# Two prepared layouts of x, pixel by pixel and in padded rows, in place of x's transposes and spread row loads

## The reference, cut to what matters

```python
# x: (4, 256, 64, 64) f32
k = conv(x, w1, padding=6, dilation=2) + b1          # 128 channels, 7x7
k = conv(k, w2) + b2                                 # 49 channels, 1x1
attn = softmax(k, axis=1)
xp = pad(x, 6)
shifts = stack([xp[:, :, 2*u:2*u+64, 2*v:2*v+64] for u in range(7) for v in range(7)], axis=1)
x = einsum('bkchw,bkhw->bchw', shifts, attn)         # layer 0 ends
h = relu(bn(conv(x, v1)))                            # 64 channels, 1x1
h = relu(bn(conv(h, v2, padding=1)))                 # 64 channels, 3x3
out = relu(bn(conv(h, v3)) + x)                      # 256 channels, 1x1
```

## Time and profile before

| | |
|---|---|
| time, median of 3 runs (lowest, highest) | 819.55 us (817.19, 820.55) |
| profiled execution: its own time / span of its instructions | 817.85 us / 816.0 us |
| granted TensorE clock, mean | 0.99 of full speed |
| busy: PE, weight loads, DVE, ACT, POOL | 96%, 88%, 81%, 47%, 43% |
| DMA | 162.17 MB in 250108 packets |

### The profile page before, as it was taken

How to read it: one execution, slowest core, us unless ns; L and a number is a source line. 1 busy time by engine, 2 the same in 40 slices (tenths; PEclk the granted TensorE clock), 3 DMA queues, 4 the chain that set the end, 5 groups by cost and what they waited for, 6 DMA issues and landing times.

```text
span 816.0 us, 13800 instructions
## 1 busy us (share of the span) xinstructions
PE 785.2 (96%) x4973; PEld 720.5 (88%) x4973; DVE 663.8 (81%) x909; ACT 381.1 (47%) x663; POOL 349.6 (43%) x253
## 2 busy tenths in 40 slices
PE   6989999999999999999999999999998999999996
PEld 2369999899999999999999999999997987777785
DVE  5998998897799588868986996888658777978896
ACT  3642212343344434444443444353425777728586
POOL 3345654484268238624852682376220012515300
PEclk9999998999999999999999999999999999999999
DMA  9951236957994899499669958784797879805598
GB/s 308 324 178 29 52 81 164 237 148 204 181 253 106 236 179 249 108 241 189 167 177 201 227 138 236 143 226 112 204 175 210 269 221 296 345 1 203 204 373 354
DMA packets 250108, 162.17 MB, mean 199 GB/s; under 512 B 191881, under 2 KB 232826, under 8 KB 247226
## 3 DMA queue, kind: packets, MB, share of 16 engines
q1 hardware_dynamic: 241322, 141.83, 67.0%
q10 hardware_dynamic: 8720, 19.47, 7.3%
HBM read 99.48 MB, written 56.36 MB: 191 GB/s over the span
## 4 chain that ended last, share of the span: by engine, by line
PE 79%; DVE 10%; issue 4%; ACT 2%; DMA 2%; POOL 1%; SPq 0%; DVEq 0%; ACTq 0%; POOLq 0%
PE ps L1338 22%; PE ps L1340 22%; PE ps L1339 22%; PE ps L1455 4%; PE ps L1505 3%; PE ps L1471 3%; DMA xbuf<-in_x 1%; DVE wsum L1828 1%; PE ps L1733 1%; DVE wpart L1828 1%; DVE whole L1878 1%; POOL ring L875 1%; PE ps L1725 1%; DMA w1raw<-in_L_conv_w 1%; DVE logit L1971 1%
## 5 line engine op out<-in xcount | busy, mean ns | idle before, releaser
L875 POOL TENSOR_TENSOR ring<-whole,ring 128x576 fp32r<-128x576 f32 x112 | 196.5, 1760 | 285.1 <-ACT ring L957 285.1
L1338 PE MATMUL ps<-w_hi,ring 128*128 128x336 f32 x832 | 276.9, 333 | 3.6 <-POOL ring L875 3.6
L1340 PE MATMUL ps<-w_hi,ring 128*128 128x336 f32 x832 | 264.3, 318 | 0.0
L1339 PE MATMUL ps<-w_lo,ring 128*128 128x336 f32 x832 | 263.1, 316 | 0.0
L1338 PEld LDWEIGHTS ps<-w_hi,ring 128*128 128x128 f32 x832 | 158.8, 191 | 9.6 <-issue 6.1
L1339 PEld LDWEIGHTS ps<-w_lo,ring 128*128 128x128 f32 x832 | 158.6, 191 | 0.0
L1340 PEld LDWEIGHTS ps<-w_hi,ring 128*128 128x128 f32 x832 | 157.8, 190 | 0.0
L957 ACT ACTIVATE ring<-whole 128x576 fp32r<-128x576 f32 x112 | 87.0, 783 | 88.0 <-POOL whole L870 45.6
L957 ACT ACTIVATE band_hi<-ps 128x320 fp32r<-128x320 f32 (+1 forms) x128 | 53.0, 418 | 125.7 <-PE ps L1455 117.6
L1338 PE MATMUL ps<-band_hi,xT_hi 128*128 128x224 f32 (+2 forms) x320 | 94.7, 296 | 2.9 <-DVE logit L1971 1.7
L1339 PE MATMUL ps<-band_lo,xT_hi 128*128 128x224 f32 (+2 forms) x320 | 92.3, 288 | 0.0
(11 more groups left out here) (229 smaller groups left out, 1360.1 us busy)
## 6 DMA issues: line engine op xcount, KB each, us to landing
xq<-in_x SPq DMA_DIRECT2D x108, 256.0 KB, 4.6
raw<-bands SPq DMA_DIRECT2D x32, 768.0 KB, 7.0
xbuf<-in_x SPq DMA_DIRECT2D x16, 1024.0 KB, 8.8
x_dram<-x ACTq DMA_DIRECT2D x31, 512.0 KB, 5.7
bands<-wide SPq DMA_DIRECT2D x64, 199.0 KB, 4.8
x1in<-x_dram SPq DMA_DIRECT2D x6, 2048.0 KB, 21.1
out<-x1in SPq DMA_DIRECT2D x12, 1024.0 KB, 3.9
bands<-wide SPq DMA_DIRECT2D x3, 1792.0 KB, 11.3
```

Source lines behind the costliest of these rows:

```text
L875: pool.tensor_tensor(split(k, 1), positions(whole[:, k % TBUFS, :], 0, 2), split(k, 0).bitcast(F32), ALU.subtract).then_inc(sig_lo_done, 1)
L1338: pe.matmul(dst, l_hi, r_hi_, start=first, stop=False, **kw)
L1339: pe.matmul(dst, l_hi, r_lo_, start=False, stop=False, **kw)
L1340: return pe.matmul(dst, l_lo, r_hi_, start=False, stop=last, **kw)
```

## The change

`kernel()` gives the program x twice. `x_rows` holds for each i the 128 partitions' 32 rows of 72 with the zeros in place, `x_pixels` holds for each step eight tiles of 128 pixels by 256 channels. In the program:

- `load_x` is one plain copy of 2310 numbers per partition. The memsets of zeros and `pads`, with the waits for them, are gone.
- `x_T` is gone on PE, with its turns of PSUM banks. `load_xp(g, pt)` loads the tile pair of part `pt` into `xp`, one of four slots (one DMA in place of two), after DVE has used what was in it; for steps 14 and 15 to the free parts of `xbuf` (`xp2`).
- ACT's `xT` copies and DVE's `xT` subtracts from `xp` or `xp2` in SBUF instead of from PSUM. Parts 2 and 3 of step 13 are split in `drain(13)` and no longer in the last half.

```diff
-        xq = sb(l0b, "xq", [P, 2, CB, 8, W])
+        xp = sb(l0b, "xp", [P, 4, 2, C])
...
+        def xp_of(g, pt):
+            return xp2(pt)[:, g - DRAIN - 1, :, :] if g > DRAIN else xp[:, pt, :, :]
...
-                src = x[n, cb * P:(cb + 1) * P].rearrange("p (r a) w -> p r a w", a=2)[:, :, a, :]
-                sp.dma_start(xflat(i)[:, 0:SH * XC].rearrange("p (r c) -> p r c", c=XC)[:, :, 2 * PAD:2 * PAD + W], src
-                             ).then_inc(x_loaded[i % XBUFS], 16)
+                sp.dma_start(xflat(i), x_rows[i]).then_inc(x_loaded[i % XBUFS], 16)
...
-                elif g == DRAIN:
-                    sp.wait_ge(xt_done, x_count(g, pt + 2))
-                elif pt >= 2:
-                    sp.wait_ge(xt_done, x_count(g, pt - 2))
-                elif g:
-                    sp.wait_ge(xt_done, x_count(g - 1, pt + 2))
+                    for i in range(2):
+                        sp.dma_start(xp2(pt)[:, i, :, :], x_pixels[g + i, 2 * pt:2 * pt + 2].rearrange("t p c -> p t c")
+                                     ).then_inc(xp2_loaded[pt], 16)
+                    return
+                if g:
+                    sp.wait_ge(xT_lo_done, x_count(g - 1, pt))
...
+                sp.dma_start(xp[:, pt, :, :], x_pixels[g, 2 * pt:2 * pt + 2].rearrange("t p c -> p t c")).then_inc(xp_loaded[pt], 16)
...
-            def pads(i):
...
             def xT(g, pt):
-                act.wait_ge(xt_done, x_count(g, pt))
+                wait_xp(act, g, pt)
                 wait_xT(act, g, pt)
-                copy(xT_pair(g, pt)[0], turn_bank("x", g, pt).rearrange("p (t c) -> p t c", c=C)).then_inc(xT_hi_done, 1)
+                copy(xT_pair(g, pt)[0], xp_of(g, pt)).then_inc(xT_hi_done, 1)
...
-            def x_T(g, pt):
...
-                    if i >= XBUFS:
-                        dve.wait_ge(pads_done, 3 * (i - XBUFS + 1))
...
-                minus(lo, turn_bank("x", g, pt).rearrange("p (t c) -> p t c", c=C), hi.bitcast(F32)).then_inc(xT_lo_done, 1)
+                minus(lo, xp_of(g, pt), hi.bitcast(F32)).then_inc(xT_lo_done, 1)
...
+    rows = x.reshape(B, CB, P, SH, 2, W).transpose(0, 4, 1, 2, 3, 5)
+    rows = np.pad(rows, [(0, 0)] * 5 + [(2 * PAD, XC - W - 2 * PAD)]).reshape(2 * PAIRS, P, SH * XC)
+    given["x_rows"] = np.pad(rows, [(0, 0), (0, 0), (0, XLEN - SH * XC)])
+    given["x_pixels"] = x.reshape(B, C, SH, 2, SW, 2).transpose(0, 3, 5, 2, 4, 1).reshape(STEPS, NT, P, C)
```

More of the change, by code:

```diff
@@ L452, in late, with xp2, wait_xp @@
             return 2 * g + h >= 2 * DRAIN - 1
-        def xq2(pt):
+        def xp2(pt):
             at = XLEN - 1024 * (2 - pt % 2)
-            place = xbuf[:, 1 + pt // 2, at:at + 1024]
-            return place.rearrange("p (k r c) -> p k r c", k=CB, c=W)
+            return xbuf[:, 1 + pt // 2, at:at + 1024].rearrange("p (i t c) -> p i t c", i=2, c=C)
+        def xp_of(g, pt):
+            return xp2(pt)[:, g - DRAIN - 1, :, :] if g > DRAIN else xp[:, pt, :, :]
+        def wait_xp(eng, g, pt):
+            if g > DRAIN:
+                eng.wait_ge(xp2_loaded[pt], 32)
+            else:
+                eng.wait_ge(xp_loaded[pt], 16 * (g + 1))
         def raw_of(g, t):
@@ L521, in x_count @@
         def x_count(g, pt):
-            if g == DRAIN - 1 and pt >= 2:
-                return 4 * g + 2 * pt - 1
-            if g == DRAIN:
-                return 4 * g + (3 + pt if pt < 2 else 2 * pt - 4)
             return 4 * g + pt + 1
@@ L739, in half @@
                 if image is not None:
-                    load_xq(image, 2)
+                    load_xp(image, 2)
                 last = q == 2 * PAIRS - 1
@@ L743, in half @@
                     for pt in range(2):
-                        load_xq(DRAIN + 1, pt)
+                        load_xp(DRAIN + 1, pt)
                 elif q % 2 == 1 and conv is not None:
@@ L765, in half @@
                     if coming:
-                        load_xq(coming, 0)
+                        load_xp(coming, 0)
                     load_raw(coming, 0)
@@ L773, in half @@
                     if coming:
-                        load_xq(coming, 1)
+                        load_xp(coming, 1)
+                    if last:
+                        load_xp(coming, 2)
                     load_raw(coming, 1)
+                    if last:
+                        load_xp(coming, 3)
                 if q == 2 * PAIRS - 1:
@@ L848, in _ @@
             pool.memset(bias[:, :], 0.0).then_inc(consts, 1)
-            for c0, c1 in ((0, 2 * PAD), (2 * PAD + W, XC)):
-                pool.memset(xbuf[:, :, 0:SH * XC].rearrange("p i (r c) -> p i r c", c=XC)[:, :, :, c0:c1], 0.0).then_inc(consts, 1)
-            pool.memset(xbuf[:, :, SH * XC:XLEN], 0.0).then_inc(consts, 1)
-            pool.wait_ge(consts, 11)
+            pool.wait_ge(consts, 8)
             for i, off in enumerate((0, 64, -64)):
@@ L1098, in image_part @@
                     xT(image, part // 3)
-                    if part == 8 and image == DRAIN - 1:
-                        xT(DRAIN, 2)
                 if part == 6:
@@ L2057, in image_part @@
                     xT(image, (2, 6, 9).index(part))
-                    if part == 9 and image == DRAIN - 1:
-                        xT(DRAIN, 2)
                 if part in (7, 8):
```

116 lines of the change are left out of this document (27 added, 89 removed).

## The result

The changed kernel takes 805.32 us (median of 4 runs, 803.32 to 806.52) against 818.73 us (817.19 to 820.55) of the kernel before on the same chip: a ratio of 0.9832, 95% interval 0.9807 to 0.9858. It gains 13.4 us where 26.7 were forecast. The profiled execution took 806.52 us, the longest of the four, at a mean granted clock of 0.982; the other three had 0.988 to 0.991.

A forecast was written before the change was run, and what follows sets the result against it. The prediction took TensorE's issue to bound the steady state: 817.85 - 26.9 (transposes) - 1.2 (start) - 0.6 + 1.0 (moved subtractions) + 1.0 (SBUF reads) = 791.1, plus 1.70 to the median, 792.8 us; range 785 to 804.

The forecast's parts named there:

- The sign and the pairs' work: Whole kernel faster, chance 0.95; in the steady pairs, TensorE's time falls from 75.2 to 71.5 us, 0.46 per transpose group.
- The start: First load of x lands sooner, so VectorE's first operation starts earlier: -1.2 us, within 0 to 1.7.
- VectorE and ScalarE read SBUF in place of PSUM: +1.0 us: In the split of x, xT_lo costs 0.4 us more each, VectorE's pair reaches 64.6 us: +1.0 us overall.
- the lock: VectorE instructions with two SBUF inputs and GpSimd instructions reading SBUF block each other: up to 1.25 us more per xT_lo.
- Only those on the chain count: 3.3% of 816.0: Over the whole span, removed TensorE transposes gain only their share of the chain of waits: -26.9 us, about 58 groups.
- the sum: All terms added to the profiled 817.85 us give 791.1; with 1.70 to the median, 792.8 us.
- The second: Rival: in the pairs VectorE and GpSimd block each other and TensorE waits; half the gain goes, 805 us; chance 0.17.
- VectorE was not the bound: Judges the slower rival: VectorE becomes the bound in the pairs, 81.4 us each, 855 us in all; chance 0.03.

The follow-up runs named there:

- e8_rows: The kernel before with the padded rows of x alone and without the memsets, its transposes kept: 818.8 us, ratio 0.9989.
- e1_psum: Changed kernel, but ScalarE copies each piece of xp into a PSUM bank and VectorE subtracts from there, except in steps 13 to 15: 802.73 us, ratio 0.9786.
- e3_xt2: Changed kernel with ScalarE's and VectorE's split of part 2 moved ahead of the softmax's end in every half: 800.36 us, ratio 0.9758.
- g2_xt2b4: As e3_xt2, and also band_lo of tile 4 moved ahead of the whole before it on VectorE: 798.32 us, ratio 0.9748.
- f2_fill: Changed kernel with four matmuls without use in place of each group of transposes, from the last half on: 809.91 us, ratio 0.9886.
- g1_fill2: Changed kernel with two matmuls without use in place of each group of transposes, from the last half on: 804.35 us, ratio 0.9834.
- e2: Changed kernel with GpSimd's operations on xbuf for a pair's first buffer moved one chunk later: 823.21 us, ratio 1.0048.
- e6: Changed kernel with the split of part 3 moved ahead of x_hi and x_lo in every half: 802.02 us, ratio 0.9798.
- e4: Changed kernel with band_lo of tiles 6 and 7 and xT_lo of part 3 ahead of the last softmax's addition: 805.75 us, ratio 0.9811.
- e5: Changed kernel with only part 3 going through a PSUM bank that ScalarE fills, as e1_psum does for all parts: 802.79 us, ratio 0.9803.
- f1: Changed kernel with SyncE waiting in the last half for the last logits' transfer before loading weights: 804.85 us, ratio 0.9814.
- f3: As e1_psum, but part 1 takes its PSUM bank behind the band of tile 3 instead of ahead of it: 806.19 us, ratio 0.9839.

## Why the prediction was wrong, point by point

- **The sign and the pairs' work: right.** A group of transposes is worth 0.45 to 0.48 us; 0.46 was read from the timeline. TensorE's work in a pair is 71.63, forecast 71.5.
- **The start: right in its mechanism, its size not clear.** VectorE's first `whole` starts at 15.18 in place of 16.75, 15.1 said. The stage is 1.4 us shorter and 1.2 in e8_rows, but the stage varies by as much between profiles of the same code; of the 1.4 us of transposes that the chain named before the first `proj`, nothing certain is seen.
- **"VectorE and ScalarE read SBUF in place of PSUM: +1.0 us" failed, by its consequence.** Its sizes were good: `xT_lo` 882 ns (0.7 to 1.1 said), VectorE's pair 63.5 (64.6 said). But I priced the delay at TensorE's tightest place and took `proj` for that place, with 1.1 us left. At `proj` 3.2 us are left in the changed kernel (`x_lo` ends at 245.84, `proj` starts at 249.03). The tightest place is the fifth unit behind it, which needs `band_lo` of tile 4 and `xT_lo` of part 2: 2.0 us of slack before the change, less than the 2.8 at `proj`, and I had not looked there. There TensorE loses 1.1 us in each pair, and the stage gained 6.0 us less than forecast. e1_psum shows that the lock is the cause of the wait, e3_xt2 and g2_xt2b4 that it is paid at one place only. And the delay did not come through `xT_lo`: in the first half of a pair, three of its four operations are as short as before; what grew was GpSimd's pair on `xbuf` (6.62 to 8.48) and the untouched `whole`, by 250 ns on average.
- **"Only those on the chain count: 3.3% of 816.0" failed from the last half on.** The chain named the transposes there, 8.1% of the drain, but work on a chain that runs along a busy engine is not yet gain: behind it waited the last softmax and the transfers of its weights, which come no sooner. With the last weights landing alike, the stage became 0.2 to 0.5 us shorter where the sum had 3.5. It became 3.0 longer because they landed 3.5 us later: the transfer of the last logits took 1.9 us more, and the last `bands<-wide` and `raw<-bands` together 13.2 us from issue to landing in place of 11.4. Why these transfers were slower is not shown.
- **The clock was not in the sum at all.** Beside the last softmax TensorE stood idle for 3.3 us and then worked at 0.50 until 612. All fourteen profiles without the transposes have such a fall, f2_fill and g1_fill2 among them, where other matmuls stand in their places, and neither of the two with them (before, e8_rows); so it goes with the change, but not simply with the missing work. The last stage lost 2.3 us with a fall behind gaps that the kernel before had too. Where the run left that stage unchanged it took 152.1 to 152.8 us in five profiles (before, e2, e3, e6, e8), 153.6 to 153.8 in two (e4, g1) and 154.9 to 155.2 in seven (the changed kernel, e1, e5, f1, f2, f3, g2). This need not be the kernel: e5_psum3 took 800.8 us twice, at a mean clock of 0.992 and 0.994, and 804.7 and 805.0 at 0.984 and 0.980. So part of the +2.3 may be the one execution that was profiled.
- **The rivals.** The second named the time (805), the mechanism and the waiting engine, and got a chance of 0.17. That its time came out is luck: it gave the lock 13 us, the halves fell 6.0 short, and the rest was the drain, its transfers and the clock; and it had TensorE waiting for `x_lo` at `proj`, where there was slack. VectorE was not the bound, with 63.5 of 72.55 us busy.

What stays open: the slow transfer of the last logits (4.75 us in two kernels, 2.7 to 2.9 in most) and of the last weights, what decides whether the clock falls in the last stage, and whether the lock accounts for the whole 1.1 us of a pair or for about half of it, as e1_psum got back.

## What to carry to other kernels

Before counting work that leaves a busy engine as gain, ask stage by stage what that engine would wait for next: in a steady loop it was all gain but at one place, in a drain that hung on transfers next to none. When an operand moves from PSUM to SBUF, price not the operation but everything in both VectorE's and GpSimd's order beside it, and follow it to the one operation that the bounding engine reaches first; moving two operations ahead of the locked ones gave more of the pair back (71.73 us) than taking the lock away through PSUM banks (72.02). And here a wait of 2.6 us on TensorE cost 4.3 to 5.7 us where the clock fell behind it, 2.8 where it did not.

## What was not expected of the hardware

- GpSimd's operation seems to be passed twice: in the changed kernel its second `xbuf` operation of the buffer, due at 242.6, took 3.97 us where the shortest takes 2.11, while VectorE's `pairs` (1.34) and `xT_lo` (0.68), which came at the same moment, ran one after the other unhindered.
- Behind a wait of 2.6 us on TensorE the granted clock fell from 1.00 in five of six pairs, to 0.71 in the pair shown (e2_clate); behind the waits of 0.9 to 1.2 us in the halves of the changed kernel and e6_xt3 it never did.
- A 128x128 f32 matmul against the identity, 0.24 us, took twice the time of the transpose of the same size, 0.12.
